# Gathered expert rows: GpSimd left with fetching alone, dot products fused on VectorE, scaling moved to ScalarE, attention scores by pairs of banks

## The chip, the cores and the metric

The kernel runs on one core of one Trainium2 chip. A core has five engines with an instruction queue each: TensorE (PE, matmuls into PSUM; its weight loads are shown as PEld), VectorE (DVE), ScalarE (ACT), GpSimd (POOL) and SyncE (SP, which issues the plain transfers). The metric is device time in microseconds, the median of several runs; lower is better. All data is fp32, except where bf16 is said.

## What is computed

Four layers over an input x of 2 x 1024 tokens with 256 features, with a context of 154 tokens per sequence. Each layer is a cross attention with 16 heads of depth 16 (layer 3: an autocorrelation in its place), then a feed-forward part of a different kind, each behind a layer norm and with a residual sum. The change touches the attention of layers 0 to 2 and the feed-forward part of layer 1:

```python
# attention, layers 0 to 2, per head
s = (x @ Wq + bq) @ (ctx @ Wk + bk).T / 4        # rotary positions in layer 2
x = x + softmax(s) @ (ctx @ Wv + bv) @ Wo + bo

# feed-forward of layer 1 (from the kernel: the reference's inputs are keys, down_embed, up_embed, w_gate, w_up, w_down)
q = norm(x) @ w_queries.T                        # 4 heads, two halves of 32
# per head: the 8 best keys of 128 for each half, the 8 best of the 64 sums, softmax -> prob[token, 4 * 8], row[token, 4 * 8]
dot = sum(norm(x)[token] * down_embed[row], features)
x  += sum(prob * gelu_like(dot) * up_embed[row], over the 32 rows)
x  += (silu(norm(x) @ w_gate.T) * (norm(x) @ w_up.T)) @ w_down.T
```

In the kernel the weight of one row is 0.5 * dot * prob * (1 + tanh(dot / 2)). Feed-forward 0 has ternary weights and a squared ReLU, 2 and 3 route to experts densely.

## The kernel before

**Tiles.** The 2048 tokens are 4 chunks (c) of 512, a chunk is 4 tiles (i) of 128 tokens on the 128 partitions. The residual stream `x_sb` stays in SBUF. All matmuls are fp32 (but for the subtraction of the maxima, bf16).

**Order.** `plan()` is a list scheduler that runs when the kernel is built. It has a cost for every step (`DUR`), the dependences, and hand-set offsets to the priorities (`PREFER`), and writes for each of the five engines an order of steps; each engine then runs its own order, held only by semaphores. The attentions come in the order (layer, chunk) = (0,0) (0,1) (1,0) (1,1) (0,2) (0,3) (1,2) (1,3) (2,0) ... (2,3), so the gathers of layer 1 run beside attention and feed-forward of other chunks and layers.

**Gather of layer 1.** Lists: `similar1` (step sm1, one for each tile, L1627 on, eight MAX8 and eight FIND_INDEX8), then `top1` (tk1) and `rows1` (ix1, four parts) for the whole chunk at once; they give `rowid` (which rows) and `prob`. A group g is 4 rows for each token of one tile; 8 groups make a tile, 32 a chunk, 128 the kernel. The rows land in `ring`, which has 20 places of 512 numbers (down row of 256, up row of 256), so 5 slots of 4. For each group:

- POOL `fetch` (gf): four indirect DMAs of 128 rows of 2 KB (L1881); it waits until the slot's earlier group is used up.
- DVE `multiply` (mu): one tensor_tensor over 1024 elements, rows times normed x, in place (L1440).
- ACT `gathered_sums` (th): four Identity activations with a sum output (L1235), then tanh (L1237).
- DVE `weights_of` (ew): two tiny operations of 128x4 (L1447, L1448).
- DVE `add_rows` (ad): three scalar_tensor_tensor, x += row * weight, each waiting for the one before (L1457 to L1459).
- ACT `weighted_rows` (sc): row 3 times its weight (L1244); POOL `add_rows` adds it to `half_sum` (L1892 for a tile's first group, L1895 for the others).
- DVE `add_half` (ga), once in a tile: x += half_sum (L1465).

POOL also adds the output bias of attention (bo: L1901, L1908).

**Attention.** A first pass takes the row maxima (p1, ph; L858, L875 on PE, L1568, L1577 on DVE). Then for two groups of heads and two parities, `score`: PE writes scores to four PSUM banks (L899, L901), ACT takes exp of banks 0,1 and of banks 2,3 (L1307), and PE starts the next parity when both are done. `score_rest` (L911, L1313) takes the last 26 context tokens, `weigh` (L924, L927) multiplies by the values, `turn_back`, `turn_out`, `project_out` (L937, L944, L954) end it.

## Time and profile before

| | us |
|---|---|
| median of 3 runs (1609.59 to 1609.88) | 1609.88 |
| profiled execution | 1606.96 |
| span of its instructions | 1605.2 |

| engine | busy us | share of the span | instructions |
|---|---|---|---|
| PE | 1290.2 | 80% | 5862 |
| DVE | 1102.5 | 69% | 2945 |
| ACT | 811.9 | 51% | 2053 |
| POOL | 692.4 | 43% | 705 |

Busy time is the union of an engine's instructions; DMA-issuing by SP, waits and semaphores don't count, POOL's indirect DMAs do. The shares are averages over three very different stages: before the first fetch (at 300.3 us), the gathers (until the last tile sum, at 1153.5 us), and layer 3 with the rest.

### The profile page before, as it was taken

To read this page: it belongs to the slowest core of one execution; us is meant where nothing else is said; L and a number is where in the kernel's file an instruction comes from. 1 tells how busy PE (TensorE), PEld (TensorE's weight loads), DVE (VectorE), ACT (ScalarE), POOL (GpSimd) and SP (SyncE) were. 2 spreads that over 40 slices of the span, in tenths; PEclk is the share of its full clock that TensorE was granted. 3 is DMA by queue.
4 is the path that set the end of the run, shared out by engine and by line. 5 is a ranking of instruction groups with operands and counts; after the bars stand their busy time and mean duration, and the time that the engine had idled before them with its cause. 6 is when DMAs were issued, how large, how long until landed. Compare 5 with 4: busy or idle time off the path is not lost.

```text
span 1605.2 us, 18853 instructions
## 1 busy us (share of the span) xinstructions
PE 1290.2 (80%) x5862; PEld 655.7 (41%) x5862; DVE 1102.5 (69%) x2945; ACT 811.9 (51%) x2053; POOL 692.4 (43%) x705
## 2 busy tenths in 40 slices
PE   4999997766779777678657676776889999999998
PEld 2345453233244434333323533442444444544544
DVE  5642418589987886998899988898863334436455
ACT  2454442756757876747557568558735341130200
POOL 2000000488888888846878778888400010010000
PEclk9799898877789889778669699989999999989999
DMA  6000000466575758634657866655310031002000
GB/s 232 24 1 0 10 1 8 86 179 162 164 165 176 196 162 222 162 106 128 176 158 172 227 167 185 180 167 167 90 24 1 0 126 34 0 27 74 1 14 27
DMA packets 59957, 168.68 MB, mean 105 GB/s; under 512 B 15760, under 2 KB 20944, under 8 KB 59216
## 3 DMA queue, kind: packets, MB, share of 16 engines
q0 software_dynamic: 40960, 134.25, 31.5%
q1 hardware_dynamic: 18896, 33.22, 6.4%
q8 instruction: 47, 0.77, 0.2%
q14 instruction: 54, 0.44, 0.1%
HBM read 162.61 MB, written 4.82 MB: 104 GB/s over the span
## 4 chain that ended last, share of the span: by engine, by line
PE 42%; POOL 21%; DVE 19%; issue 10%; ACT 4%; DMA 3%; SPq 0%; DVEq 0%; POOLq 0%; ACTq 0%
POOL bufR L1881 18%; PE psum L1210 7%; PE psum L1072 5%; PE psum L1084 3%; POOL half_sum L1895 3%; PE psum L1154 2%; PE psum L1129 2%; DVE bufB L1568 2%; DMA bufR<-in_table,rowid 2%; PE psum L820 2%; PE psum L1007 2%; DVE bufR L1440 2%; PE psum L954 2%; PE psum L999 2%; DVE x_sb L1458 1%
## 5 line engine op out<-in xcount | busy, mean ns | idle before, releaser
L1881 POOL DMA_INDIRECT bufR<-in_table,rowid x512 | 559.1, 1092 | 227.9 <-issue 121.3
L1235 ACT ACTIVATE bufR<-bufR 128x256 f32<-128x256 f32 x512 | 205.5, 405 | 61.2 <-DVE bufR L1440 60.7
L1440 DVE TENSOR_TENSOR bufR<-bufR 128x1024 f32<-128x1024 f32 x128 | 161.2, 1262 | 53.7 <-DMA bufR<-in_table,rowid 53.5
L1072 PE MATMUL psum<-xtf,wf 128*128 128x512 f32 x320 | 153.0, 622 | 16.0 <-DVE x_sb L1734 13.1
L1244 ACT ACTIVATE bufR<-bufR,ew 128x256 f32<-128x256 f32 x128 | 63.8, 504 | 133.6 <-DVE ew L1448 133.5
L1503 DVE TENSOR_TENSOR x_sb<-x_sb,psum 128x256 f32<-128x256 f32 x128 | 50.6, 416 | 115.7 <-PE psum L1007 69.0
L858 PE MATMUL psum<-bufB 32*128 32x308 f32 x576 | 71.2, 571 | 63.7 <-DVE bufB L1568 50.0
L1908 POOL TENSOR_TENSOR x_sb<-x_sb,wattn 128x256 f32<-128x256 f32 x16 | 11.1, 728 | 254.9 <-DMA wattn<-in_attn 147.7
L1901 POOL TENSOR_TENSOR x_sb<-x_sb,wattn 128x256 f32<-128x256 f32 x32 | 22.7, 741 | 220.4 <-DMA wattn<-in_attn 140.4
L1841 DVE SCALAR_TENSOR_TENSOR x_sb<-psum,bufR,x_sb 128x256 f32<-128x256 f32 x128 | 61.9, 483 | 74.6 <-PE psum L1210 69.8
L1084 PE MATMUL psum<-wf,bufR 128*128 128x256 f32 x320 | 84.1, 411 | 34.3 <-DVE bufR L1725 34.3
L1568 DVE TENSOR_REDUCE bufB<-psum 128x8 f32<-128x1232 f32 x72 | 102.6, 1433 | 10.6 <-PE psum L858 10.1
L1307 ACT ACTIVATE bufR<-psum 128x1024 f32<-128x1024 f32 x96 | 92.7, 1018 | 23.4 <-PE psum L901 23.0
L1072 PEld LDWEIGHTS psum<-xtf,wf 128*128 128x128 f32 x320 | 60.5, 198 | 95.4 <-issue 65.0
L1895 POOL TENSOR_TENSOR half_sum<-half_sum,bufR 128x256 f32<-128x256 f32 x112 | 89.7, 801 | 18.5 <-ACT bufR L1244 16.3
L1235 ACT ACTIVATION_READ_ACCUMULATOR bufR<-bufR 128x1 f32 x512 | 96.8, 189 | 0.0
L1734 DVE SCALAR_TENSOR_TENSOR x_sb<-psum,bufR,x_sb 128x256 f32<-128x256 f32 x128 | 53.0, 476 | 52.7 <-PE psum L1084 52.7
L1084 PEld LDWEIGHTS psum<-wf,bufR 128*128 128x128 f32 x320 | 62.8, 203 | 61.4 <-issue 53.4
L899 PE MATMUL psum<-bufB 32*128 32x512 f32 x384 | 62.9, 727 | 22.5 <-ACT bufR L1307 15.3
L1261 ACT ACTIVATE xa<-x_sb,shift,rstd 128x256 f32<-128x256 f32 x112 | 57.9, 589 | 42.2 <-DVE shift L1500 42.2
L1458 DVE SCALAR_TENSOR_TENSOR x_sb<-bufR,ew,x_sb 128x256 f32<-128x256 f32 x128 | 73.2, 571 | 4.6
L1459 DVE SCALAR_TENSOR_TENSOR x_sb<-bufR,ew,x_sb 128x256 f32<-128x256 f32 x128 | 69.1, 540 | 4.6
(240 smaller groups left out, 2528.5 us busy)
## 6 DMA issues: line engine op xcount, KB each, us to landing
bufR<-in_table,rowid POOLq DMA_INDIRECT x512, 4.3
wf<-in_ffn SPq DMA_DIRECT2D x2, 2304.0 KB, 14.9
bufR<-in_ffn SPq DMA_DIRECT2D x1, 2696.5 KB, 16.8
wattn<-in_attn SPq DMA_DIRECT2D x4, 641.0 KB
wf<-in_rope SPq DMA_DIRECT2D x4, 512.0 KB, 6.2
bufB<-in_ffn SPq DMA_DIRECT2D x1, 2048.0 KB, 8.4
scr_corr<-bufR SPq DMA_DIRECT2D x16, 128.0 KB, 2.3
bufR<-scr_corr SPq DMA_DIRECT2D x4, 512.0 KB, 4.6
```

The costliest lines, as they stand in the source:

```text
L858: ins = mm(psum[:, at + z, 0:PAR * S], q[r, g, i * P:(i + 1) * P], keysm[r, g, b, :, 0:S], start=True, stop=True)
L1072: ins = mm(bank(6 + r), gu[:, kt, r, :], xtf[:, kt, :], start=kt == 0, stop=kt == KT - 1)
L1084: ins = mm(psum[:, (4 if c == LAST else 6) + i // 2, i % 2 * D:(i % 2 + 1) * D], hm2[:, GUS.index(m) % 7, i * P:(i + 1) * P], down2[:, m, ...
L1210: ins = mm(bank(unit_bank3(c, y)), xt_of("z", c)[:, kt, i * P:(i + 1) * P], we3[:, kt, e * 512:(e + 1) * 512], start=kt == 0, stop=kt == K ...
L1235: own.mark(act(row, row, ACT.Identity, accum_out=dots[:, g % 4, j:j + 1]))
L1307: act(probs[side][:, par:4:2, :], psum[:, 2 * side:2 * side + 2, :], ACT.Exp).then_inc(at_ex, 1)
L1440: tt(rows, rows, cast(xg[c % 2][:, i, :].unsqueeze(1), [P, GRP, D]), ALU.mult).then_inc(f1_mu, 1)
L1458: own.link(stt(x, ring[:, at + 1, D:2 * D], ew[:, g % 4, 1:2], x, ALU.mult, ALU.add))
L1459: stt(x, ring[:, at + 2, D:2 * D], ew[:, g % 4, 2:3], x, ALU.mult, ALU.add).then_inc(f1_acc, 1)
L1568: eng.reduce_max(m4[:, i, :].rearrange("p (z r) -> p z r", z=BANDS)[:, :, PAR * g:PAR * g + PAR], psum[:, at:at + BANDS, 0:PAR * S].rearra ...
L1881: eng.indirect_dma_start(ring[:, s * GRP + j, :], None, io["table"], bass.IndirectOffsetOnAxis(ap=rowid[c % 2][:, at + j:at + j + 1], axis ...
L1895: eng.tensor_tensor(half_sum[:, :], half_sum[:, :], up, ALU.add).then_inc(f1_half, 1)
```

## The change

- The dot products: `multiply` is now four tensor_tensor_reduce of 256 elements, each with its sum as a second output; ACT keeps the tanh alone.
- All four up rows of a group are scaled on ACT. DVE adds them in one tensor_tensor of 1024 elements to a new buffer `wide` of 4 x 256 (the first two groups of a tile are added to each other, so 7 such sums in a tile); `add_sum` folds it 512 + 256 wide and adds it to x, once in a tile. POOL's `add_rows` is gone, and a slot is free only when DVE's wide sum has run.
- The lists of chunk 0 are made in two halves of two tiles; rows and probabilities have a semaphore each.
- Attention scores run by sides: PE fills banks 0,1, then 2,3, and refills a side once ACT has taken exp of that side. DVE's `turn_back` gets a wait on the third `weigh`.
- New costs and new offsets, so all five orders are new. The SBUF reserved for the software DMA descriptors is set to 8192 bytes a partition.

```diff
             def fetch(g):
...
                 if g >= SLOTS:
-                    eng.wait_ge(f1_acc, g - SLOTS + 1)
+                    eng.wait_ge(f1_acc, added(g - SLOTS))
                 for j in range(GRP):
-                    if g >= SLOTS and j == GRP - 1:
-                        eng.wait_ge(f1_half, g - SLOTS + 1)
                     eng.indirect_dma_start(ring[:, s * GRP + j, :], None, io["table"],
-            def add_rows(g):
-                at = GRP * (g % SLOTS)
-                up = ring[:, at + 3, D:2 * D]
-                eng.wait_ge(f1_wt, g + 1)
...
-                    eng.tensor_tensor(half_sum[:, :], half_sum[:, :], up, ALU.add).then_inc(f1_half, 1)
             def multiply(g):
-                rows = ring[:, at:at + GRP, 0:D]
-                tt(rows, rows, cast(xg[c % 2][:, i, :].unsqueeze(1), [P, GRP, D]), ALU.mult).then_inc(f1_mu, 1)
+                for j in range(GRP):
+                    row = ring[:, at + j, 0:D]
+                    eng.tensor_tensor_reduce(row, row, xg[c % 2][:, i, :], 1.0, 0.0, ALU.mult, ALU.add, dots[:, g % 4, j:j + 1])\
+                        .then_inc(f1_mu, 1)
+            def added(g):
+                return g // NG * (NG - 1) + max(g % NG, 1)
             def add_rows(g):
-                own.link(stt(x, ring[:, at, D:2 * D], ew[:, g % 4, 0:1], x, ALU.mult, ALU.add))
-                own.link(stt(x, ring[:, at + 1, D:2 * D], ew[:, g % 4, 1:2], x, ALU.mult, ALU.add))
-                stt(x, ring[:, at + 2, D:2 * D], ew[:, g % 4, 2:3], x, ALU.mult, ALU.add).then_inc(f1_acc, 1)
+                eng.wait_ge(f1_wt, GRP * (g + 1))
+                if g % NG == 1:
+                    if g > 1:
+                        eng.wait_ge(f1_tile, g // NG)
+                    tt(wide[:, :, :], weighted(g - 1), weighted(g), ALU.add).then_inc(f1_acc, 1)
+                else:
+                    eng.wait_ge(f1_acc, added(g - 1))
+                    tt(wide[:, :, :], wide[:, :, :], weighted(g), ALU.add).then_inc(f1_acc, 1)
-            def add_half(g):
-                tt(x, x, half_sum[:, :], ALU.add).then_inc(f1_tile, 1)
+            def add_sum(g):
+                own.link(tt(wide[:, 0:2, :], wide[:, 0:2, :], wide[:, 2:4, :], ALU.add))
+                own.link(tt(wide[:, 0, :], wide[:, 0, :], wide[:, 1, :], ALU.add))
+                eng.wait_ge(f1_x, g // NG + 1)
+                tt(x, x, wide[:, 0, :], ALU.add).then_inc(f1_tile, 1)
-            def gathered_sums(g):
-                for j in range(GRP):
-                    row = ring[:, at + j, 0:D]
-                    own.mark(act(row, row, ACT.Identity, accum_out=dots[:, g % 4, j:j + 1]))
-                own.wait()
+            def tangent(g):
                 act(thalf[:, g % 4, :], dots[:, g % 4, :], ACT.Tanh, scale=0.5).then_inc(f1_th, 1)
             def weighted_rows(g):
-                for j in (3,):
+                for j in range(GRP):
                     row = ring[:, at + j, D:2 * D]
-                    ins = act(row, row, ACT.Copy, scale=ew[:, g % 4, j:j + 1])
-                ins.then_inc(f1_wt, 1)
+                    act(row, row, ACT.Copy, scale=ew[:, g % 4, j:j + 1]).then_inc(f1_wt, 1)
+def lists_of(c):
+    return (TI // 2, TI) if c == 0 else (TI,)
             def score(layer, c, g, par, side):
-                for z in range(BANDS):
+                for z in (2 * side, 2 * side + 1):
                     mm(bank(z), keysm[band(z), g, b, par, 0:P], q[band(z), g, :], start=True, stop=False)
-                for z in range(BANDS):
+                for z in (2 * side, 2 * side + 1):
                     ins = mm(bank(z), sel[band(z), 2 * g + par, :], mt[band(z), :], start=False, stop=True)
                 ins.then_inc(at_s2, 1)
-    nc = _bacc.Bacc("TRN2", target_bir_lowering=False, num_devices=1)
+    nc = _bacc.Bacc("TRN2", target_bir_lowering=False, num_devices=1, dynamic_dma_scratch_size=8192)
```

## Rows read from the trace of the kernel before

**Rows 1.** Busy time in three stretches: us, then each engine, PE clock, DMA, GB/s.
```profile
0.00:300.30 300.30, 254.16 (x1242) 129.05 (x1246) 150.61 (x462) 126.14 (x199) 14.36 (x33) 0.90 0.10 37
300.30:1153.50 853.20, 610.90 (x2679) 313.33 (x2672) 736.96 (x1829) 568.26 (x1666) 667.00 (x656) 0.84 0.63 169
1153.50:1605.20 451.70, 425.18 (x1946) 213.31 (x1944) 214.92 (x656) 117.47 (x189) 11.05 (x16) 0.97 0.10 30
```
**Rows 2.** The chain that ended last, by engine (the page, part 4).
```profile
PE 42%; POOL 21%; DVE 19%; issue 10%; ACT 4%; DMA 3%; SPq 0%; DVEq 0%; POOLq 0%; ACTq 0%
```
**Rows 3.** POOL's groups, 300.3 to 1153.5: busy, mean ns | idle before, releaser.
```profile
L1881 POOL DMA_INDIRECT bufR<-in_table,rowid x512 | 559.1, 1092 | 227.9 <-issue 121.3 <-DVE prob L1684 81.3 <-POOL half_sum L1895 12.8
L1895 POOL TENSOR_TENSOR half_sum<-half_sum,bufR 128x256 f32<-128x256 f32 x112 | 89.7, 801 | 18.5 <-ACT bufR L1244 16.3
```
**Rows 4.** DVE's groups that belong to the gather, 300.3 to 1153.5.
```profile
L1440 DVE TENSOR_TENSOR bufR<-bufR 128x1024 f32<-128x1024 f32 x128 | 161.2, 1262 | 53.7 <-DMA bufR<-in_table,rowid 53.5
L1458 DVE SCALAR_TENSOR_TENSOR x_sb<-bufR,ew,x_sb 128x256 f32<-128x256 f32 x128 | 73.2, 571 | 4.6
L1457 DVE SCALAR_TENSOR_TENSOR x_sb<-bufR,ew,x_sb 128x256 f32<-128x256 f32 x128 | 69.4, 542 | 1.7 <-DVE ew L1448 0.3
L1459 DVE SCALAR_TENSOR_TENSOR x_sb<-bufR,ew,x_sb 128x256 f32<-128x256 f32 x128 | 69.1, 540 | 4.6
L1447 DVE SCALAR_TENSOR_TENSOR ew<-dots,prob 128x4 f32<-128x4 f32 x128 | 29.2, 228 | 5.2 <-ACT thalf L1237 5.1
L1448 DVE SCALAR_TENSOR_TENSOR ew<-thalf,ew 128x4 f32<-128x4 f32 x128 | 26.7, 209 | 4.4
```
**Rows 5.** Single lines: duration ns min/median/max, first and last start us, shape.
```profile
L1440 DVE TENSOR_TENSOR bufR<-bufR x128: 1207/1218/2228, 309.7 to 1144.8; 128x1024 f32<-128x1024 f32 x128
L1458 DVE SCALAR_TENSOR_TENSOR x_sb<-bufR,ew,x_sb x128: 483/485/1447, 324.4 to 1151.7; 128x256 f32<-128x256 f32 x128
L1447 DVE SCALAR_TENSOR_TENSOR ew<-dots,prob x128: 143/155/1169, 312.9 to 1150.5; 128x4 f32<-128x4 f32 x128
L1465 DVE TENSOR_TENSOR x_sb<-x_sb,half_sum x16: 400/420/426, 378.2 to 1153.1; 128x256 f32<-128x256 f32 x16
L1881 POOL DMA_INDIRECT bufR<-in_table,rowid x512: 942/959/1984, 300.3 to 1138.1; - x171
```
**Rows 6.** Timeline around two collisions of DVE and POOL: start us, us, instruction.
```profile
426.17 1.31 DVE L1459 SCALAR_TENSOR_TENSOR x_sb<-bufR,ew,x_sb 128x256 f32<-128x256 f32 x1
426.45 0.73 POOL L1895 TENSOR_TENSOR half_sum<-half_sum,bufR 128x256 f32<-128x256 f32 x1
...
433.28 1.30 DVE L1674 TENSOR_TENSOR bufR<-bufR 128x1024 f32<-128x1024 f32 x1
...
433.67 1.77 POOL L1881 DMA_INDIRECT bufR<-in_table,rowid  x1 [0.16 <-POOL half_sum L1892]
```
**Rows 7.** Busy time in one stretch of 100 us, columns as in Rows 1.
```profile
400.00:500.00 100.00, 76.77 (x328) 35.27 (x328) 94.15 (x234) 67.39 (x198) 82.90 (x80) 0.85 0.63 166
```
**Rows 8.** DVE's timeline: second tile searched, lists of chunk 0 begun, last list step.
```profile
268.82 0.29 DVE L1644 FIND_INDEX8 bufR<-bufR,psum 128x8 uint32<-128x128 f32 x1
...
280.41 0.29 DVE L1653 CAST bufR<-bufR 128x256 f32<-128x256 uint32 x1
...
299.74 0.29 DVE L1684 TENSOR_TENSOR prob<-work 128x128 f32<-128x128 f32 x1
```
**Rows 9.** ACT's groups of the gather, 300.3 to 1153.5.
```profile
L1235 ACT ACTIVATE bufR<-bufR 128x256 f32<-128x256 f32 x512 | 205.5, 405 | 61.2 <-DVE bufR L1440 60.7
L1235 ACT ACTIVATION_READ_ACCUMULATOR bufR<-bufR 128x1 f32 x512 | 96.8, 189 | 0.0
L1244 ACT ACTIVATE bufR<-bufR,ew 128x256 f32<-128x256 f32 x128 | 63.8, 504 | 133.6 <-DVE ew L1448 133.5
```
**Rows 10.** Longest waits, 300.3 to 1153.5: PE for ACT's exp (us, times, longest).
```profile
PE psum L899 <- ACT bufR L1307: 14.4, 7, 5.5
```
**Rows 11.** DMA issues (page, part 6): names, queue, count, us from issue to landing.
```profile
bufR<-in_table,rowid POOLq DMA_INDIRECT x512, 4.3
```

245 lines of the change are left out of this document (134 added, 111 removed), and 4 rows, old and new, of the table DVE.

## The prediction, made before the changed kernel ran

> **What bounds the kernel now.** I read the busy times by stretch first, cut at the first fetch and at the last tile sum [rows 1]. Before 300.3 us PE is busy for 254 of 300 us, after 1153.5 us for 425 of 452: both ends are PE's. The 853 us between are not: PE has 611. Two other engines are nearly full there. POOL is busy for 667 us, and between indirect DMAs that follow each other stand 121 us that are not counted as busy [rows 3]: 0.3 us for each of the 384 and some that come straight behind another. Together 788 of 853 us. DVE is busy for 737, 86%. The chain that ended last agrees: POOL 21% and "issue" 10%, mostly those gaps, so some 500 us of it lie on POOL [rows 2]. So in the middle POOL sets the pace, DVE is a close second, and what the change is worth is decided by how far DVE lets it go.
>
> **POOL.** Removed: 112 adds of 0.801 us and 16 copies; all that is not fetching is 667.0 - 559.1 = 108 us [rows 1, 3], of which 89.7 are those adds; some 12 us of bias adds stay. Left: 512 fetches x (1.092 + 0.3) = 713, + 12 = 725 us. If POOL stayed the bound, the middle would be 110 to 128 us shorter. It can't, as DVE's sum shows.
>
> **DVE, a price that vanishes.** The gather's rows cost 161.2 + 73.2 + 69.4 + 69.1 + 29.2 + 26.7 = 428.8 us, and 16 x 0.42 = 6.7 for the tile sums [rows 4, 5]: 435.5. By their medians it would be 128 x (1.218 + 3 x 0.485 + 2 x 0.155) = 381.8, + 6.7 = 388.5 [rows 5], with the median of the one small step for both. The 47 us between are long instances such as the scalar_tensor_tensor of 1.31 us that has POOL's add of 0.73 us within it [rows 6]. The other way round, a fetch takes 1.77 instead of 0.96 us beside a wide tensor_tensor of DVE. So the adds on POOL hold DVE up, and DVE holds the fetches up but isn't held by them. With no adds on POOL I take DVE at its medians. The Trainium skill ("SBUF — State Buffer", Who interferes with whom) says that a DVE instruction with two SBUF inputs and a GpSimd instruction that reads SBUF exclude each other for a whole instruction. By that rule the trace agrees, and the fetches stay slow, since the changed DVE work has two SBUF inputs throughout; 1.092 us for one stays in my sum.
>
> **DVE, the new work.** Four tensor_tensor_reduce a group stand nowhere in the trace. The lower bound for one is a plain tensor_tensor of 256 elements, 0.42 [rows 5]; the nearest row is the fused scalar_tensor_tensor with two SBUF tensors, 0.485; the upper bound adds a separate read-out of the sum as ACT's has, 0.189 [rows 9]: 0.674. I take 0.485: 512 x 0.485 = 248 us. The small steps: 256 x 0.155 = 40. Wide sums: 7 in each of 16 tiles, 112 x 1.218 = 136. Tile sums: 512, 256 and 256 wide, with 0.00104 us for an element (between 0.42 at 256 and 1.218 at 1024) 0.69 + 0.42 + 0.42, x 16 = 24. Together 448, against 435.5 now: the fused form and POOL's share cost DVE next to nothing, only because the collisions go.
>
> **Lists in halves.** Two tiles are searched at 269.1 us, all four at 280.4, and the lists take from there to 300.0 [rows 8]. Half of them behind the second tile is 9.8 us and about 1 of fixed costs: the first fetch at 280 instead of 300.3. The other searches and the second half, some 19 us of DVE, then fall into the middle. All later lists are unchanged.
>
> **ACT.** Out: 205.5 + 96.8 us; in: 384 x 0.504 = 194 [rows 9]. ACT falls from 568 to 460 us in the middle [rows 1] and is no bound. It is now in line before the wide sum: the path of a group from landing to a free slot is 1.94 + 0.2 (tanh, like a small step) + 0.31 + 2.0 (four scalings) + 1.2 = 5.7 us without queues.
>
> **Attention by sides.** The waits for exp that it can shorten cost PE 14.4 us in the middle [rows 10]. PE isn't the bound there, so I take 0; if they all counted, 14. The new waits of DVE's turn_back are on a matmul that the plan puts ahead of it; queued behind it would be DVE's gather steps. I take 0 and bound it by 10. A reserve for descriptors is now 8192 bytes: no row shows what it did before. The fetches in flight are few, so I take 0, with no other bound than a chance below.
>
> **The sum.** DVE in the middle: 737.0 - 435.5 = 301.5 of other work, + 448 + 19 = 768.5 us. DVE can't be filled wholly: the best stretch of 100 us before has 94% [rows 7]. 768.5 / 0.94 = 818 us from 280, so the last tile sum falls at 1098 instead of 1153.5: -56. POOL needs only 725 of them and waits for slots. The start is shorter only by what the halves give, counted already; the end stays at 452 us, as its PE is full and nothing there is changed. Span 1605.2 - 56 = 1549, execution (1.8 more, as before) 1551, and the median of the runs lies 2.9 above the profiled execution: 1554. At 90% full instead the middle takes 854 us: 1590; at 97%, 792: 1528. That is the forecast's own range.
>
> **Rival 1, the other side: the fused product is dear.** One mechanism: tensor_tensor_reduce on fp32 pays for its sum. The gain of 56 x 0.94 = 52 us of DVE is gone when one costs 0.485 + 52 / 512 = 0.59 us. At 0.674 it is 97 us of DVE more, 103 of time: 1657. For it: ACT's form of the same sum is two instructions. Against it: scalar_tensor_tensor already does two operations for each element in 0.485. The Trainium skill ("Vector Engine (DVE) Microarchitecture Reference", Points that are easy to get wrong) has a rule by which this whole family of instructions halves its rate on two fp32 SBUF sources, as no port is left for the accumulator. Worked out from rows: 0.485 + 256 x 0.00104 = 0.75 us, 136 us more of DVE, 1554 + 145 = 1699. The scalar_tensor_tensor here doesn't run at half rate, but it gives out no sum, so the trace doesn't settle that. 10%, nearly all on the first price.
>
> **Rival 2, the slots.** A slot is now free only after the scaling and the wide sum, for a tile's first group only with the second's. 5.6 for fetching + 4.3 landing [rows 11] + 5.7 = 15.6 us, + 6.4 = 22 for the first, against 5 x 6.4 = 32 us of ring. The 10 us left go when DVE is busy with a search of four us at two of the three steps. Half a us lost for each group is 64 us: 1618 at worst, some 1600 likely. Against it: POOL waited for slots hardly at all before. 11%.
>
> **Rival 3, faster: the new plan unloads DVE.** DVE has 237 us free behind the gathers [rows 1]. If 40 to 60 us of its other work are put there, and the fused product costs 0.42 (33 us less), the middle falls towards POOL's 725 + about 15 for the last group: 280 + 740 = 1020, 1476 at the very best; 1490 to 1530 likely. Against it: PE, 94% full there, must take the matmuls of that work too. 24%.
>
> **Rival 4, it doesn't do what it says.** Fetches become slower by the smaller reserve or by DVE's denser two-input work: from 1.092 by 0.2 us is 102 us, POOL 827 + 15, again the bound and about 1578; only far above that does it lose. 3%.
>
> **How the numbers follow.** The forecast has 52%: 1554 us. The range takes in rival 3's likely part and rival 2's, and leaves out rival 1: 1500 to 1610. Measurements of this kernel can tell about 0.2%, 3 us, from no change. Faster by more: 52 + 24 + most of rivals 2 and 4 = 85%; within: 4%; slower: rival 1 and the end of rival 2, 11%.
>
> **What would show it.** Right: first fetch near 280; the fused product near 0.485; the wide sum at 1.22 with no instances above 2 us; DVE over 92% busy in the middle; POOL with idle time put down to DVE's wide sum. Wrong: DVE under 88% there with POOL waiting (rival 2), a product over 0.59 (rival 1), DVE with clearly less than 770 us in the middle (rival 3).

## The result and the profile after

The changed kernel takes 1588.69 us (median of 4 runs, 1582.45 to 1590.08) against 1609.88 before in the same comparison (1609.59 to 1611.26): a ratio of 0.986, 95% interval 0.983 to 0.989. That is 21 us less, where 56 were forecast. In a second comparison, against 1616.67, the ratio was 0.983 (0.978 to 0.988). The profiled executions have spans of 1605.2 and 1588.1 us, 17 us apart. Lines are those of the changed kernel from here on: L1930 is the fetch, L1472 the fused product, L1273 the scaling, L1493 and L1496 the wide sums, L1501 to L1504 the tile sum, L933 and L935 the scores, L1728 the last step of a list's row numbers.

The first view is the busy time in the same three stretches as [rows 1]: to the first fetch, to the last tile sum, and to the end (us, then PE, its weight loads, DVE, ACT, POOL, the PE clock, the share of the DMA engines, GB/s).

```profile
0.00:279.80 279.80, 239.16 (x1148) 123.07 (x1150) 134.35 (x384) 114.09 (x184) 14.38 (x33) 0.89 0.11 40
279.80:1133.80 854.00, 651.25 (x2752) 324.58 (x2749) 706.81 (x2575) 504.51 (x1029) 554.98 (x528) 0.84 0.70 169
1133.80:1588.10 454.30, 431.88 (x1965) 216.54 (x1963) 216.78 (x662) 119.84 (x191) 11.03 (x16) 0.96 0.11 30
```

The start is 20.5 us shorter, the end stage 2.6 us longer, and the middle, where all the work was taken out, is 0.8 us longer than before: 854.0 against 853.2. So the whole net gain lies before the first fetch. POOL has 112 us less to do in the middle, DVE 30 less, ACT 64 less, and PE 40 more. DVE is busy for 83% of the middle; before it was 86%, and the forecast had 94%. By the chain that ended last (the page, part 4), POOL is still on the path, with the gaps between its DMAs ("issue") beside it; [rows 2] had 21% and 10%:

```profile
PE 47%; DVE 18%; POOL 18%; issue 9%; DMA 5%; ACT 3%; DVEq 0%; SPq 0%; ACTq 0%
```

The gather's groups in the middle (busy us, mean ns of one | idle before it and what ended it), beside [rows 3, 4, 9]:

```profile
L1472 DVE CUSTOM_DVE_ANT_0 bufR<-bufR 128x256 f32<-128x256 f32 x512 | 189.2, 425 | 82.4 <-DMA bufR<-in_table,rowid 82.3
L1472 DVE DVE_READ_ACCUMULATOR2_ANT dots<- 128x1 f32 x512 | 41.5, 81 | 0.0
L1496 DVE TENSOR_TENSOR wide<-wide,bufR 128x1024 f32<-128x1024 f32 x96 | 116.9, 1218 | 6.7 <-ACT bufR L1273 6.2
L1930 POOL DMA_INDIRECT bufR<-in_table,rowid x512 | 541.8, 1058 | 336.6 <-issue 147.5 <-DVE rowid L1728 100.0 <-DVE wide L1496 46.4
L1273 ACT ACTIVATE bufR<-bufR,ew 128x256 f32<-128x256 f32 x512 | 216.0, 497 | 117.3 <-DVE ew L1482 116.8
```

The 100.0 us that POOL waited for the lists are two waits of 50.0: one ends with the first fetch and lies ahead of the middle, the other is taken up below.

A fused product is shown as two instructions, the product and a read-out of its sum. Each has a long duration, 425 and 81 ns, but the timeline shows that they overlap (start us, us, instruction):

```profile
500.73 0.42 DVE L1472 CUSTOM_DVE_ANT_0 bufR<-bufR 128x256 f32<-128x256 f32 x1 [1.82 <-DMA bufR<-in_table,rowid]
501.08 0.08 DVE L1472 DVE_READ_ACCUMULATOR2_ANT dots<- 128x1 f32 x1
501.08 0.42 DVE L1472 CUSTOM_DVE_ANT_0 bufR<-bufR 128x256 f32<-128x256 f32 x1
```

The next product starts 0.35 us after the last one did. So the four of a group take 1.5 us, and the union of all 1024 instructions of this line is 190 us of DVE, not the 248 of the sum. All of the gather's rows on DVE together cover 380 us (their union, worked out from the starts and ends of the trace); 707 - 380 = 327 us is other work, against 301.5 + 19 in the sum.

The durations of single lines (ns min/median/max, first and last start) show what became of the collisions of [rows 6]:

```profile
L1472 DVE CUSTOM_DVE_ANT_0 bufR<-bufR x512: 404/421/994, 292.2 to 1127.0; 128x256 f32<-128x256 f32 x171
L1496 DVE TENSOR_TENSOR wide<-wide,bufR x96: 1201/1216/1232, 309.9 to 1131.0; 128x1024 f32<-128x1024 f32 x96
L1930 POOL DMA_INDIRECT bufR<-in_table,rowid x512: 942/949/2002, 279.8 to 1121.8; - x171
```

The wide sum has no long instance: its maximum is 16 ns above its median, where the tensor_tensor of the same size had 2228 ns in [rows 5]. The fetches are still drawn out, up to 2.0 us. POOL keeps 16 adds of the output bias in the middle (L1938), and where they meet fused products, these are drawn out as well. It happens to four products, 0.93 to 0.99 us each, with four bias adds of 0.9 us beside them:

```profile
647.57 0.99 DVE L1472 CUSTOM_DVE_ANT_0 bufR<-bufR 128x256 f32<-128x256 f32 x1
648.17 3.57 POOL L1938 TENSOR_TENSOR x_sb<-x_sb,wattn 128x256 f32<-128x256 f32 x4
```

**Who waits.** The longest waits of DVE and POOL in the middle (us in total, times, longest):

```profile
DVE bufR L1472 <- DMA bufR<-in_table,rowid: 82.3, 41, 7.1
...
POOL bufR L1930 <- DVE rowid L1728: 50.0, 1, 50.0
POOL bufR L1930 <- DVE wide L1496: 46.4, 15, 12.4
POOL bufR L1930 <- DVE wide L1493: 42.6, 10, 12.7
```

DVE waits 82 us for rows that are still on their way, and POOL waits 89 us for slots that DVE hasn't freed. Both happen in the same kernel at different moments: neither engine is full, and neither waits for the other all the time. POOL also waits 50 us at one place, which is the start of chunk 2. POOL's timeline there, first of the kernel before, then of the changed one:

```profile
706.76 0.94 POOL L1881 DMA_INDIRECT bufR<-in_table,rowid  x1 [0.31 <-issue]
713.41 0.73 POOL L1895 TENSOR_TENSOR half_sum<-half_sum,bufR 128x256 f32<-128x256 f32 x1 [5.71 <-ACT bufR L1244]
730.94 0.96 POOL L1881 DMA_INDIRECT bufR<-in_table,rowid  x1 [16.80 <-DVE prob L1684]
```

```profile
674.23 0.95 POOL L1930 DMA_INDIRECT bufR<-in_table,rowid  x1 [0.30 <-issue]
725.20 0.95 POOL L1930 DMA_INDIRECT bufR<-in_table,rowid  x1 [50.02 <-DVE rowid L1728]
```

The last fetch of chunk 1 comes 32.5 us earlier than before, 20.5 of which are the earlier start. The lists of chunk 2 come only 5.7 us earlier; by the plan they hang on attention and feed-forward of that chunk. So 27 us that the gather had gained are waited away at 675 to 725 us. Cut at the first fetch of each chunk, the changed kernel has this (columns as above):

```profile
279.80:481.20 201.40, 150.64 (x644) 70.49 (x644) 172.67 (x680) 119.89 (x236) 140.31 (x137) 0.80 0.73 169
481.20:725.20 244.00, 194.12 (x874) 97.09 (x869) 191.10 (x696) 150.93 (x312) 140.01 (x136) 0.83 0.65 154
725.20:931.60 206.40, 150.10 (x651) 80.63 (x651) 181.57 (x658) 110.22 (x226) 135.09 (x129) 0.85 0.73 184
931.60:1133.80 202.20, 156.39 (x590) 76.37 (x589) 161.46 (x544) 123.47 (x258) 139.56 (x128) 0.87 0.70 170
```

The same four of the kernel before are 202.6, 228.0, 208.5 and 214.1 us long. DVE at 94% is nowhere: 86, 78, 88 and 80%.

### The profile page after: what moved, and what is told of

It is laid out like the page before. It is cut to its first block, busy times and chain, and to the rows that moved or that the text cites. A ratio compares the mean times of both kernels' runs of the same rounds, so it can differ in the third digit from the quotient of the medians.

```text
span 1588.1 us, 18855 instructions
## 1 busy us (share of the span) xinstructions
PE 1322.3 (83%) x5862; PEld 664.2 (42%) x5862; DVE 1057.9 (67%) x3619; ACT 738.4 (46%) x1404; POOL 580.4 (37%) x577
## 4 chain that ended last, share of the span: by engine, by line
PE 47%; DVE 18%; POOL 18%; issue 9%; DMA 5%; ACT 3%; DVEq 0%; SPq 0%; ACTq 0%
POOL bufR L1930 18%; PE psum L1244 7%; PE psum L1106 6%; DMA bufR<-in_table,rowid 4%; PE psum L1118 3%; PE psum L933 3%; DVE bufR L1472 3%; PE psum L1163 2%; PE psum L1188 2%; PE psum L843 2%; PE psum L891 2%; PE psum L1033 2%; DVE bufB L1607 2%; DVE wide L1496 2%; PE psum L1041 2%
## 5 line engine op out<-in xcount | busy, mean ns | idle before, releaser
L1930 POOL DMA_INDIRECT bufR<-in_table,rowid x512 | 541.8, 1058 | 336.6 <-issue 147.5
L1273 ACT ACTIVATE bufR<-bufR,ew 128x256 f32<-128x256 f32 x512 | 216.0, 497 | 117.3 <-DVE ew L1482 116.8
L1472 DVE CUSTOM_DVE_ANT_0 bufR<-bufR 128x256 f32<-128x256 f32 x512 | 189.2, 425 | 82.4 <-DMA bufR<-in_table,rowid 82.3
L1106 PE MATMUL psum<-xtf,wf 128*128 128x512 f32 x320 | 153.1, 623 | 16.5 <-DVE x_sb L1785 14.0
L1496 DVE TENSOR_TENSOR wide<-wide,bufR 128x1024 f32<-128x1024 f32 x96 | 116.9, 1218 | 6.7 <-ACT bufR L1273 6.2
L933 PE MATMUL psum<-bufB 32*128 32x512 f32 x384 | 93.0, 759 | 28.7 <-ACT bufR L1334 21.7
L1118 PE MATMUL psum<-wf,bufR 128*128 128x256 f32 x320 | 89.5, 431 | 20.0 <-DVE bufR L1776 19.9
L1938 POOL TENSOR_TENSOR x_sb<-x_sb,wattn 128x256 f32<-128x256 f32 x32 | 24.3, 790 | 215.9 <-DMA wattn<-in_attn 155.2
L1118 PEld LDWEIGHTS psum<-wf,bufR 128*128 128x128 f32 x320 | 66.3, 215 | 50.9 <-issue 41.4
L891 PEld LDWEIGHTS psum<-bufB 32*128 32x128 f32 x576 | 27.9, 226 | 99.3 <-DVE bufB L1607 67.3
L1776 DVE TENSOR_TENSOR bufR<-bufR,psum 128x512 f32<-128x512 f32 x40 | 27.3, 683 | 62.3 <-ACT bufR L1390 62.3
L1072 PE MATMUL psum<-xtf,wf 128*128 128x512 f32 x128 | 64.5, 650 | 2.8 <-DVE bufR L1689 2.8
L1033 PE MATMUL psum<-xtf,wf 128*128 128x512 f32 x128 | 64.8, 634 | 0.3 <-issue 0.2
```

What stands on the lines that cost most here:

```text
L891: ins = mm(psum[:, at + z, 0:PAR * S], q[r, g, i * P:(i + 1) * P], keysm[r, g, b, :, 0:S], start=True, stop=True)
L933: mm(bank(z), keysm[band(z), g, b, par, 0:P], q[band(z), g, :], start=True, stop=False)
L1033: ins = mm(bank(6 + m % 2), fc_t[:, kt, m * P:(m + 1) * P], xtf[:, kt, :], start=kt == 0, stop=kt == KT - 1)
L1106: ins = mm(bank(6 + r), gu[:, kt, r, :], xtf[:, kt, :], start=kt == 0, stop=kt == KT - 1)
L1118: ins = mm(psum[:, (4 if c == LAST else 6) + i // 2, i % 2 * D:(i % 2 + 1) * D], hm2[:, GUS.index(m) % 7, i * P:(i + 1) * P], down2[:, m, ...
L1273: act(row, row, ACT.Copy, scale=ew[:, g % 4, j:j + 1]).then_inc(f1_wt, 1)
```

## The experiments

All kernels of one comparison ran on one chip beside the kernel before. "Old order" is the order of the kernel before, "new order" that of the changed kernel; a kernel with one of them differs from its parent in nothing but what is said.

### One part of the change at a time

**Scores by sides, alone, in the old order.**

```diff
-                for z in range(BANDS):
+                for side in range(2):
...
+                    for z in (2 * side, 2 * side + 1):
+                        mm(bank(z), keysm[band(z), g, b, par, 0:P], q[band(z), g, :], start=True, stop=False)
```

> The kernel before, its own order of steps, with one part of the change alone: TensorE writes the scores of banks 0,1 and signals, then those of banks 2,3, back to back, and refills each pair when ScalarE has left it. Theory S (scores by pairs of banks cost TensorE time, since two instead of four groups of 32 rows of the array work side by side): TensorE busy rises by 25 to 35 us from 1290 to some 1320, the score lines L899 and L901 from 84 to about 120 us, and the time rises by 5 to 20 us over before. Rival O (the split is free and only shortens the waits for exp; the lost gain lies in the lists and the order of steps): TensorE busy stays within 5 us of 1290, the time is the same or up to 15 us shorter.

Measured: 1610.63 against 1613.46, ratio 0.997 (0.995 to 1.000): a gain at the edge of what can be told. PE is busy for 1302.2 us against 1290.2, 12 us more. That is less than theory S said and more than rival O allows; the time is as O has it.

**The sides undone in the changed kernel, in the new order** (three of four passes fill all four banks again).

> The changed kernel, its own order of steps, with the scores of all four banks written at once again in three of four passes (the pass that starts the second group of heads stays split, as its order needs it). Theory S: TensorE busy falls by some 20 to 25 us from 1322, time 10 to 20 us below the changed kernel's 1588. Rival O: TensorE busy as it was, time the same, or longer by up to 15 us, as exp and scores no longer overlap.

Measured: 1613.67, ratio 1.000 (0.997 to 1.004). Without the sides the changed kernel loses nearly all of its gain, some 23 us, more than either theory had. The scores of the changed kernel and of the kernel before, on PE:

```profile
L933 PE MATMUL psum<-bufB 32*128 32x512 f32 x384 | 93.0, 759 | 28.7 <-ACT bufR L1334 21.7 <-ACT bufB L1325 4.2 <-ACT bufR L1344 2.8
L935 PE MATMUL psum<-bufB 32*128 32x512 bf16 x192 | 32.3, 428 | 0.0
```

```profile
L899 PE MATMUL psum<-bufB 32*128 32x512 f32 x384 | 62.9, 727 | 22.5 <-ACT bufR L1307 15.3 <-ACT bufR L1317 3.8 <-ACT bufB L1297 3.4
L901 PE MATMUL psum<-bufB 32*128 32x512 bf16 x192 | 21.2, 417 | 0.0
```

The busy times of the two lines overlap, so they can't be added. Their union (worked out from the starts and ends of the trace) is 75 us before and 110 us in the changed kernel. The matmuls are the same, each of nearly the same duration, but fewer of them run beside each other. In the kernel before four start within 0.02 us (at 402.36 us), in the changed one two do (at 401.92 us), and the next two 0.9 us later. Only a part of this is the sides' own: they alone make it 82 us in the old order, where both sides are issued behind each other. In the new order the joined kernel has 92 us, and PE is busy for 1306.3 us in it, 16 less than in the changed kernel.

The sides pay all the same, and the stages of the joined kernel show where:

```profile
0.00:289.40 289.40, 239.12 (x1148) 122.48 (x1150) 134.38 (x384) 113.79 (x184) 14.36 (x34) 0.88 0.11 38
289.40:1144.40 855.00, 635.45 (x2754) 318.97 (x2751) 706.51 (x2575) 503.90 (x1029) 550.05 (x528) 0.85 0.74 168
1144.40:1610.10 465.70, 431.75 (x1965) 218.06 (x1963) 216.66 (x662) 119.80 (x191) 11.02 (x16) 0.96 0.10 29
```

The start is 9.6 us longer than in the changed kernel, the end stage 11.4, and the middle only 1.0. In the joined form PE waits 52 us for ACT's exp, against 28 in the changed kernel (over the whole span):

```profile
PE psum L941 <- ACT bufR L1344: 31.1, 16, 6.1
PE psum L955 <- ACT bufR L1344: 20.6, 16, 3.2
```

Of these 52 us, 40 lie in the middle, which is no longer for them. In the start there are 8.7, which fits its 9.6 us. In the end stage there are only 2.3, so what makes that stage longer stays open.

So the worth of the sides depends on the order around them: 3 us in the old one, 23 in the new one, and nothing of it in the middle. The prediction's 0 came from the old order's 14 us [rows 10], which are waits of the middle alone.

**The reserve of 8192 bytes, alone, in the kernel before** (one execution).

> The kernel before with nothing changed but the space reserved for the software DMA descriptors, 8192 bytes. If the reserve doesn't bind: fetches at 1.09 us and 4.3 us from issue to landing, time within 3 us of before. If it does: landing near the changed kernel's 4.9 us or fetches longer, and a longer time.

Measured: 1606.14 in one execution, where the kernel before took 1604 to 1622 us in the same comparison. A fetch takes 1.082 us in the mean, against 1.092 before, and lands after 4.3 us as before: the reserve does nothing that one execution can show.

**The adds of GpSimd left out, nothing put in their place, in the old order.**

```diff
             def add_rows(g):
-                at = GRP * (g % SLOTS)
...
+                pass
```

> The kernel before in its own order, with GpSimd's 112 adds and 16 copies left out: the fourth up row of every group is missing from the sum (half_sum is zero and still added). It frees GpSimd of 108 us in the middle and takes away the collisions with VectorE (47 us), and changes nothing else. By the prediction's reasoning (VectorE's busy time sets the middle): 690 us of VectorE at 94% are 734 us against 853, GpSimd 725 + 15 = 740, so about 1610 - 113 = some 1495 to 1510. Theory L, that the lists of the third chunk set when its fetches begin, whatever GpSimd and VectorE could do in between: the third chunk begins at 715 to 731 as before, GpSimd's wait there grows from 17 to 50 us or more, and only the last two chunks gain: 20 to 45 us, 1565 to 1590. No long instances of the scalar_tensor_tensor by both.

Measured: 1559.95, ratio 0.968 (0.964 to 0.971), so 52 us less. This is the cleanest test of the prediction's reasoning, since no other cost is in play, and the time lies outside the range of both expectations. The middle of this kernel in one line:

```profile
301.10:1108.60 807.50, 607.95 (x2678) 310.81 (x2671) 689.31 (x1829) 566.49 (x1666) 566.91 (x528) 0.85 0.71 178
```

And the durations of one of DVE's three short adds, whose maximum was 1447 ns in [rows 5]:

```profile
L1458 DVE SCALAR_TENSOR_TENSOR x_sb<-bufR,ew,x_sb x128: 483/485/864, 323.8 to 1107.0; 128x256 f32<-128x256 f32 x128
```

DVE went from 737.0 to 689.3 us: the price of the collisions, 47 us in the sum, was 48. But the middle went from 853 to 807, and not to 734, as DVE at 94% would have it: DVE is at 85%, near the 86% of before. The third chunk (chunk 2) began at 712.3, 18.6 us earlier than in the kernel before. That speaks against theory L in its strict form (715 or later) as much as against the prediction: the lists came earlier when everything else did.

**The new form of the gather, alone, in the old order** (no halves, no sides, but the reserve of 8192 bytes).

```diff
-                tt(rows, rows, cast(xg[c % 2][:, i, :].unsqueeze(1), [P, GRP, D]), ALU.mult).then_inc(f1_mu, 1)
+                for j in range(GRP):
+                    row = ring[:, at + j, 0:D]
+                    eng.tensor_tensor_reduce(row, row, xg[c % 2][:, i, :], 1.0, 0.0, ALU.mult, ALU.add, dots[:, g % 4, j:j + 1])\
...
-                own.link(stt(x, ring[:, at, D:2 * D], ew[:, g % 4, 0:1], x, ALU.mult, ALU.add))
...
+                    tt(wide[:, :, :], wide[:, :, :], weighted(g), ALU.add).then_inc(f1_acc, 1)
```

> The kernel before in its own order with the new form of the gather alone: fused products and wide sums on VectorE, scaling of four rows on ScalarE, no adds on GpSimd (three tile sums are swapped with the wide sum next to them). No halves of lists, no sides, no new order. By the prediction's sum, without the halves: VectorE 301.5 + 448 = 749.5 at 94% = 797 us from 300.3, last tile sum near 1098, 1610 - 56 = 1554. Theory C (no engine's total sets the middle, but the turns that gather, lists and attention take in each engine's order): leaving the adds out altogether gave 1560, and VectorE now carries more per group and frees the slot later than three short adds did, so 10 to 30 us of that are given back: 1570 to 1590. Over 1600 if the old order is unfit for the longer way to a free slot.

Measured: 1642.29, ratio 1.019 (1.015 to 1.023): 30 us slower than before, as the last of the expectations has it. The heart of the change is a loss where the old order is kept. The whole loss lies in the middle (302.1 to 1190.1 us): it is 35 us longer than in the kernel before, though DVE has only 691.9 us to do in it, against 737.0, and is busy for 78%. The longest waits between 281 and 1260 us:

```profile
DVE wide L1466 <- ACT bufR L1242: 100.1, 71, 3.7
...
POOL bufR L1893 <- DVE wide L1463: 90.1, 14, 14.5
POOL bufR L1893 <- DVE wide L1466: 49.9, 15, 8.0
```

The wide sum (L1466 here) can only run when ACT has scaled all four rows, and in the old order it stands, in 84 of 112 cases, right behind the weights or with one step between. So DVE, with everything else queued behind it, waits 100 us for ACT. The prediction had seen that ACT now stands in line before the wide sum, and gave it a latency, but no price on DVE. In the new order there are mostly two to four steps between, and the same wait is 6.2 + 2.5 us. That this wait is what makes the kernel slower isn't shown: POOL waits 140 us for slots beside it, and the next run takes the wait away without a gain.

**The same with each wide sum one step of the gather later in DVE's order.**

> The new gather in the old order (1642 there, with VectorE 100 us in wait for ScalarE's four scalings), with one thing moved: each wide sum stands one step of the gather later in VectorE's order (behind the next product or the next weights). Theory W: that wait, for which the prediction had no price, is what makes the new form slower in the old order, and the new order takes it away by placing the sum later: VectorE's wait for the scaling falls from 100 to under 40 us, the time by 25 to 60 us: 1582 to 1617. Rival: the slot is now free later, GpSimd's waits for wide sums (140 us) grow by what the other wait loses: 1630 to 1650.

Measured: a ratio of 1.065 (1.060 to 1.070), 1748.29 us, on a chip on which the kernel before took 1641. In that chip's traces engines stood still for several microseconds with nothing in the profile that ends the wait, so the size isn't to be compared with the others. The waits between 281 and 1260 us are these; some of POOL's may belong to the standstills:

```profile
DVE wide L1466 <- ACT bufR L1242: 25.4, 11, 10.8
...
POOL bufR L1905 <- DVE wide L1466: 122.2, 23, 12.8
POOL bufR L1905 <- DVE wide L1463: 118.3, 14, 21.5
```

DVE's wait fell, as theory W has it, but the gain that W had from it didn't come, and POOL's waits for slots grew from 140 to 240 us: the rival's mechanism. The kernel lost more than the rival had, and how much of that is the chip's isn't known. A later sum spares DVE and starves POOL. Only this one shift was tried.

### What the middle is short of

**Six slots instead of five, in the new order.**

```diff
-RING, GRP = 20, 4
+RING, GRP = 24, 4
```

The reserve for descriptors is 4096 bytes here, which wasn't run by itself.

> The changed kernel, its own order of steps, with six slots for gathered rows instead of five (24 places of 512 numbers; the reserve for descriptors is 4096 bytes). The slot waits of GpSimd, 89 us in 25 waits in the changed kernel, should fall under 30 us. Theory L (the middle is set by the lists of chunk 2, which come at 725 us whatever the fetches do, so waits for slots before them cost nothing): time 5 to 12 us below the changed kernel, all of it behind 725 us. Rival 2 of the prediction (slots set the pace): 25 us or more below, and the lists of chunk 2 earlier too. If neither: the same time, with the waits turned into waits of VectorE for rows.

Measured: 1569.49 (1567.71 to 1575.32), ratio 0.973 (0.967 to 0.978), 19 us less than the changed kernel; this version beats both. Its waits between 281 and 1260 us:

```profile
DVE bufR L1472 <- DMA bufR<-in_table,rowid: 41.9, 24, 5.2
...
POOL bufR L1930 <- DVE wide L1496: 29.4, 11, 11.4
POOL bufR L1930 <- DVE wide L1493: 20.3, 4, 11.2
```

One more slot nearly halves both waits at once, POOL's for slots from 89 to 50 and DVE's for rows from 82 to 42 us. It takes away no work at all (DVE 708.6 us in the middle, against 706.8), and the middle is 23 us shorter (830.9 us). So the slots couple the two engines. The gain lies between theory L's 5 to 12 us and rival 2's 25 or more, and the slot waits stayed above the 30 us that were expected. DVE is at 85% even so: the slots are a part of what the forecast missed, and not all of it.

**The fetches of chunk 2 don't wait for their own lists** (they use the row numbers of chunk 1; own order of DVE kept).

```diff
-                    eng.wait_ge(f1_idx, listed(c, at // GRP // NG * len(lists_of(c)) // TI))
+                    eng.wait_ge(f1_idx, listed(1 if c == 2 else c, at // GRP // NG * len(lists_of(c)) // TI))
```

> The changed kernel in its own order; only the fetches of chunk 2 use the row numbers of chunk 1 (wrong rows, same work), so GpSimd fills the ring of chunk 2 while VectorE still makes its lists. VectorE's order keeps its first product behind the lists. Theory L (the 50 us in which GpSimd waits for these lists are worth their fetches): the first fetch of chunk 2 at 675 instead of 725, five groups are there when the lists are ready, and all later fetches are 20 to 28 us earlier: 1560 to 1569. Theory C: the later fetches come up sooner to slots that VectorE frees in its turns with the attention, so only part is kept: 1570 to 1582. If the lists don't matter: 1585 to 1590.

Measured: 1580.05, ratio 0.979 (0.976 to 0.982), 9 us less than the changed kernel. The wait of 50 us is gone, five groups lie ready, and only 9 us come out of it. POOL's waits for slots grew from 89 to 128 us (80.4 + 47.3). Theory C's range held, and theory L's did not: POOL's wait for the lists is where earlier gains show up, but it is not what sets the time. This run leaves DVE's first product of chunk 2 behind the lists. Whether the lists themselves hold up DVE it can't show. That they don't come at a fixed time, other runs do: chunk 2 is first fetched at 725 us in the changed kernel, and at 694 with fewer fetches (below).

**An order made anew, with fetches of chunks 2 and 3 by the lists before them, and one with six slots and chunk 2's lists in halves.** For both the offsets were fitted again against the planner's own costs.

> The changed kernel; chunks 2 and 3 fetch by the rows and probabilities of the chunk before (wrong rows, same amount of work), so that their first fetch waits for no list of their own. Their lists are still made. New order and refitted offsets. Theory L (the lists of chunk 2 gate): the third chunk begins at 675 to 700 instead of 725, GpSimd's wait of 50 us is gone, the time falls by 20 to 45 us: 1545 to 1568. Theory D (VectorE's amount of work sets the middle): the work is the same, the third chunk begins earlier but the slots come free later, 1580 to 1600. Theory S (slots): the ring holds GpSimd up throughout, waits for the wide sum rise from 89 us by what the list wait loses, 1575 to 1590.

Measured: 1616.22, ratio 1.003 (1.000 to 1.006).

> The changed kernel with six slots instead of five (known to the planner), the lists of chunk 2 in halves like those of chunk 0, a reserve of 2048 bytes for descriptors, new order and refitted offsets. Six slots alone gave 1569.5. Theory L: the third chunk's first fetch comes some 10 us earlier against its last tile's search, so 1550 to 1562. Theory D: halves only move VectorE's work, no gain over six slots alone: 1566 to 1576. Slower than 1580 only if the new order is worse by itself.

Measured: 1604.82, ratio 0.996 (0.993 to 0.998).

The first lies outside every range of its expectations. The second is above 1580, which its expectation had for a new order that is worse by itself. Both are inconclusive for what they were made for. The third chunk did begin at 680 in the first, yet both are slower than their parents by 28 and 35 us. The second has the six slots and halves besides, and should have been at 1569 or under. Fetching ahead and six slots made a kernel faster where its order was kept, so the new order is the likely cause (the second also has a reserve of 2048 bytes, which wasn't run by itself). Then an order fitted to the planner's costs can be 30 us worse than another. It is of the size of the whole effect that was to be predicted.

### Taking work from one engine

Four kernels, in the new order, on one chip. "Fewer products": one fused product in four is left (173 us less of DVE by the groups' times; its busy time in the middle fell by 130 us, from 708.5 to 578.1). "Fewer fetches": from group 5 on three rows in four are fetched, 123 x 1.36 = 167 us less of POOL with the gaps.

```diff
-                for j in range(GRP):
+                for j in range(1):
                     row = ring[:, at + j, 0:D]
                     eng.tensor_tensor_reduce(...
...
-                for j in range(GRP):
+                for j in range(GRP if g < SLOTS else GRP - 1):
                     eng.indirect_dma_start(...
```

> The changed kernel itself, as the corner of a square of four that run on one chip (itself, fewer products, fewer fetches, both). The time of the kernel before differed from chip to chip (1641 in the last comparison against 1610 to 1613), so the corners have to be compared on the same one. Expected ratio to the kernel before: 0.986, as measured, if the ratio doesn't depend on the chip; 0.99 to 1.00 if a slower chip takes some of the gain.

> The corner with one fused product in four (173 us less of VectorE), as measured once at a ratio of 0.966. Expected again: 31 us (25 to 37) under the changed kernel of the same chip. On a chip that is slower in what neither engine does (landings, the way from one engine to the next), the gain is smaller: 10 to 25 us.

> The corner with three fetches in four (167 us less of GpSimd), as measured once at a ratio of 0.953. Expected again: 52 us (45 to 59) under the changed kernel of the same chip, or 20 to 45 on a slower one.

> The corner with both cuts. In turns on each other: the gains add, 75 to 95 us under the changed kernel. Next bound behind each other: 110 to 160 us. The same stretches: 55 to 75 us, or no more than the fetches alone (about 52), in which case VectorE's products only ever cost what they delay the slots by.

| kernel | us | ratio to before | under the changed kernel |
|---|---|---|---|
| the changed kernel | 1586.37 | 0.983 (0.978 to 0.988) | |
| fewer products | 1555.97 | 0.966 (0.961 to 0.971) | 30 |
| fewer fetches | 1533.91 | 0.952 (0.947 to 0.958) | 52 |
| both | 1509.92 | 0.936 (0.932 to 0.941) | 76 |

Each cut had been measured before on other chips, with these expectations. The times were 1557.44 and 1536.89, and the ratios nearly the same, 0.966 (0.963 to 0.970) and 0.953 (0.950 to 0.955):

> The changed kernel in its own order, with one fused product in four (dots of the other three rows are zero): 384 fused products less, 384 x 0.45 = 173 us less of VectorE in the middle, nothing else changed. Theory D (VectorE sets the middle): the middle falls to what GpSimd needs, 725 + 15, plus the wait for lists of 50: last tile sum near 1070 and less, 1500 to 1520. Theory L with slots: slots come free earlier, so the waits for wide sums (89 us) go to under 30, the lists of chunk 2 come 5 to 20 us earlier: 1535 to 1560. If neither VectorE nor slots matter and PE and its chain set everything: 1580 to 1590.

> The changed kernel in its own order; from group 5 on only three of a group's four rows are fetched, and VectorE and ScalarE do the fourth row's product and scaling on other data (wrong result, same work). GpSimd has 123 fetches less, 123 x 1.36 = 167 us. Taking 173 us from VectorE gave 31 us. If GpSimd is no bound any more, as the prediction has it (VectorE sets the middle): 0 to 15 us, 1574 to 1589. Theory P (GpSimd's fetches are still what the rest waits for over most of chunks 0, 1 and 3, with VectorE waiting 82 us for landings): 40 to 80 us, 1509 to 1549. Theory C, where it is one of several in turns: 15 to 40 us, 1549 to 1574.

The gains nearly add: 30 + 52 = 82, and both together give 76. That is the lower end of what was expected of gains that add, and a small overlap can't be told from none. Were DVE the bound, as the prediction had it, fewer fetches would have given nothing; they give the more of the two. Their 52 us lie in theory P's range, in which the fetches are still what the rest mostly waits for, and above theory C's. Were one the next bound behind the other, both together would have given far more than the sum. A us taken from POOL is worth 0.31 us of time, one taken from DVE 0.23 of its busy time. The waits of "fewer products" (first fence) and of "fewer fetches" (second) between 281 and 1260 us show where the rest of each cut goes:

```profile
DVE bufR L1472 <- DMA bufR<-in_table,rowid: 132.8, 53, 7.5
```

```profile
POOL bufR L1932 <- DVE wide L1498: 134.8, 45, 16.1
POOL bufR L1932 <- DVE wide L1495: 71.6, 15, 14.4
```

A lighter DVE waits longer for rows (133 us instead of 83), and a lighter POOL waits longer for slots (206 us instead of 83 on this chip). Each hands its free time to the other as a wait.

**Both cuts, the first time.**

> Both cuts at once in the changed kernel's own order: three of four fetches and one of four fused products (wrong result). Alone they gave 52 us (of 167 taken from GpSimd) and 31 us (of 173 taken from VectorE). If the two wait on each other in turns (a ring of five slots, orders written beforehand), the gains add: 75 to 95 us, 1494 to 1514. If each alone had only met the other as the next bound, both together give far more: 110 to 160 us, 1429 to 1479. If both shorten the same stretches (a wait for the other engine's work that neither shortens sets the rest), less than the sum: 55 to 75 us, 1514 to 1534.

Measured: 1596.93, ratio 0.974 (0.969 to 0.979), on the chip with 1641 us for the kernel before. A wait of this kind stood nowhere in the other chips' traces; the profile names no line that ends it:

```profile
DVE bufB L1609 <- remote: 19.5, 5, 6.0
```

It is inconclusive, and what that chip had remains open. The four kernels on one chip took its place.

**Less work for PE**: half of the matmuls left out of feed-forward 0 for chunks 2 and 3, of layer 1's gate, up and down, and of layer 2's gate and up for two chunks.

> The changed kernel in its own order with some 92 us less of PE in the middle: half of the matmuls are left out of feed-forward 0 for chunks 2 and 3, of the gate, up and down matmuls of layer 1, and of gate and up of layer 2 for its first two chunks (wrong result; everything else is unchanged). Theory P (fetches): PE is hidden, 0 to 15 us, 1574 to 1589. Theory C: PE is one of those that take turns, 20 to 45 us, 1544 to 1569. If PE's chain sets the middle: 60 to 92 us, 1497 to 1529.

Measured: 1589.50, ratio 0.987 (0.984 to 0.990): no difference to the changed kernel. Its middle:

```profile
281.30:1132.50 851.20, 585.16 (x2466) 282.91 (x2463) 706.65 (x2575) 506.15 (x1031) 557.91 (x528) 0.78 0.69 169
```

PE's busy time there fell by 66 us, less than the 92 that the expectation had estimated. Its granted clock in the middle was 0.78 instead of 0.84, a mean between the two levels of 1.2 and 2.4 GHz, and matmuls that were left as they are took longer (L933 875 ns in the mean against 805). How much of the difference is the clock's isn't shown. PE is hidden in the middle, at either amount: theory P's range held, and theory C fell in so far as it counted PE among those that take turns.

## Why the prediction missed, step by step

The sign was right, and 1588.69 lies in the range of 1500 to 1610. The forecast was 35 us too low: 56 us of gain were 21. The start came as forecast; the 35 us are the middle, which was to fall from 853 to 818 us and stayed at 854.

- **What bounds the kernel now: half right.** POOL was on the path, and the four kernels on one chip say that it still is, more than DVE. Wrong is the frame, in which a middle has one pace-setter, and the next engine takes over when the first is relieved. With five slots and an order written beforehand POOL and DVE wait on each other in turns, and a us saved on either is worth a fifth to a third.
- **"DVE at 94%" is the step that failed** (768.5 / 0.94 = 818 us for the middle). 94% was the best stretch of 100 us [rows 7]. The changed kernel has 83%, the one without GpSimd's adds 85%, the one with six slots 708.6 / 830.9 = 85%. At 83% the work found, 707 us, fills 854; at 94% it would have filled 752. This term alone costs 102 us, and the next one hid 66 of them. The mean of the middle before, 737.0 / 853.2 = 86% [rows 1], would have been no forecast either: with the 768.5 us of the sum it gives 889 us, and with the 707 that were found it gives 818 again. So the fill of DVE isn't a number that can be carried from one kernel to the next. It was 71% with fewer products and 89% with fewer fetches. What the waits show in its place is that DVE stands for rows and POOL for slots. Six slots give back 19 of the 35 us; the rest of the cause stays open.
- **Luck: "at 90% full instead the middle takes 854 us: 1590".** Both numbers are within 1.5 us of what was measured, but by two errors that cancel, 62 us too much work and a fill that is 7 points too high.
- **DVE's work: 707 us, not 768.5.** Nearly the whole difference of 62 us is the fused product, 190 us against 248. 0.485 us was taken for one, between bounds of 0.42 and 0.674. The duration in the trace is 0.425 + 0.081, but the spacing is 0.35: below the lower bound, which was the duration of a plain tensor_tensor. Durations were multiplied by counts where instructions overlap at their ends. Rival 1 (a dear product) fell. The Trainium skill ("Vector Engine (DVE) Microarchitecture Reference", Points that are easy to get wrong) says of the form `S2S2D2_STT` that two SBUF sources that aren't bf16 halve its rate. The fused product isn't at half rate here: 0.42 us for 256 elements, as for the plain form. The profile shows it as CUSTOM_DVE_ANT_0, and no run here shows whether that is the form that the page means.
- **The wide and small steps: right.** 1.218 us for a wide sum, as in [rows 5]; 0.157 and 0.162 for the small ones against 0.155; the tile sum 0.69, 0.43, 0.43 against 0.69, 0.42, 0.42.
- **The collisions: right.** 47 us were to go, and the run without adds lost 48 us of DVE. The rule that was cited from the Trainium skill ("SBUF — State Buffer", Who interferes with whom) stays in agreement: with the adds gone from GpSimd no wide sum is drawn out, the four fused products that meet its bias adds are, and fetches beside DVE's two-input work still reach 2.0 us. A fetch takes 1.058 us in the mean, where the sum had 1.092.
- **The lists in halves: the right number at the start, in part by luck, and wrong behind it.** The first fetch came at 279.8, forecast 280. The sum had the second tile searched at 269.1 us and 9.8 and about 1 for the lists; it was 267.1 and 12.7. But in the joined kernel, with the same halves and the same order, the second tile is searched at 276.6 and the first fetch comes at 289.4. So 9.6 of the 20.5 us need the sides, which were put at 0. "All later lists are unchanged" was taken as "unchanged and in time". The kernel before already waited 16.8 us for the list of chunk 2, in a row of which only the sum was read (81.3 in two waits [rows 3]); now it is 50.0. With c0 and c1 faster by 12 us and the start by 20.5, 27 of these 32 us are waited for there. The run that takes the wait away shows that it is worth no more than 9 by itself, and that waits for slots grow in its place.
- **The scaling in line before the wide sum: priced at nothing on DVE.** In the old order DVE waits 100 us for it, and there the new form of the gather turns the gain of 52 us for GpSimd's adds into a loss of 30. That the wait is the cause isn't shown (above). The forecast held the order for neutral, but by these runs the new order, with halves and sides, is worth 1642 - 1588 = some 54 us (ratios 1.019 and 0.986). By stages these are 22 us of the start and 34 of the middle. As the sides do nothing in the middle, the 34 belong to the order and the halves. How much of that is order alone wasn't measured.
- **ACT: 505 us, not 460**, for the same reason as the product. The sums and read-outs that went are 205.5 + 96.8 = 302 us by their groups [rows 9], but they overlapped. The timeline of the kernel before shows it, three rows below each other 0.40 us from one activation to the next:

```profile
404.41 0.40 ACT L1235 ACTIVATE bufR<-bufR 128x256 f32<-128x256 f32 x1
404.71 0.19 ACT L1235 ACTIVATION_READ_ACCUMULATOR bufR<-bufR 128x1 f32 x1
404.81 0.40 ACT L1235 ACTIVATE bufR<-bufR 128x256 f32<-128x256 f32 x1
```

  The busy time of that line alone is 217 us in the middle of the kernel before, and 217 + 64 - 216 = 65 us less of ACT is what the change brings (64 measured). It didn't matter for the time, but it stood in the trace before the prediction, and would have warned of the same sum for DVE.
- **Attention by sides: 0 forecast, 23 us in the new order, 3 in the old.** The bound given, 14 us, was read from waits of the old order and of the middle, while the sides pay before and behind it, where the prediction itself has PE as the bound. PE is busy for 32 us more in the changed kernel, 16 of them by the sides; that wasn't foreseen.
- **The end stage and the reserve: right within 3 us**, 454.3 against 451.7 us, and 1606 with the reserve alone.
- **Rival 2 (slots), 11% and 1600 us, named a part of the mechanism**, and its sign came: DVE under 88% with POOL waiting. The sign of rival 3, clearly less than 770 us of DVE, came too, but from the cheap product. Rival 2's path of 15.6 us without queues was right in its parts, but a slot of the changed kernel is held for 26.8 us in the mean over the 128 groups (worked out from the starts and ends in the trace), of a ring of five. 9.7 of these are between the last fetch and the first product, 4.7 between the products and the scaling, and 4.1 between the scaling and the end of the wide sum, where it is 9.8 for a tile's first group, which waits for the second's. It was set aside with "POOL waited for slots hardly at all before". That was a row of a kernel whose POOL seldom caught up with the ring (9.4 us of waits for DVE's adds).
- **Rival 3 (the plan unloads DVE) fell**: hardly any work of DVE went behind the gathers, 216.8 us there against 214.9.

Open remain the worth of the halves and of the order each by itself, what holds DVE at 85% with six slots, and how much a better order could give with five.

## What to carry to other kernels

Where two engines pass buffers round a short ring in an order fixed beforehand, don't sum one engine's work and divide by a fill, the best one least of all: DVE's fill of the middle was anywhere from 71 to 89% in these kernels, by what the other engine had to do. Look for waits in both directions (each engine waiting for the other at different moments). Here a fifth to a third of what was taken from either came out as time. Look at what one buffer more does (19 us here), before any engine is made faster. Compare by stages: here the middle that was worked on gained nothing, and what was gained came from the start. A step that gets a new engine in line before it has to be priced in the order that it stands in: the new form of the gather was 2% slower in the old order, and 1% faster in the new one, with halves and sides.

## What the hardware showed that was not expected

- Fused products with a sum follow each other every 0.35 us, though each is shown with 0.42 us and its read-out with 0.08. Durations on DVE are not additive at this size.
- Matmuls on 32 rows run beside each other when they stand on different row bands: four at a time the 384 + 192 score matmuls kept PE busy for 75 us, mostly two at a time for 110, each with nearly the same duration (0.73 and 0.76 us).
- With some 290 of 2750 matmuls left out of a stretch of 850 us, PE's granted clock there was 0.78 instead of 0.84, and its busy time only 66 us less.
- A fused product of 0.42 us took 0.93 to 0.99 us beside GpSimd's adds, in the four cases in which they met.
- The kernel before took 1610 to 1617 us in five comparisons (three chips, and one that isn't named) and 1641 on one more chip, and a changed kernel's loss there was out of proportion (1597 for a kernel that took 1510 elsewhere). Kernels that are to be compared have to run on one chip.
